# First attention's context as one fp32 product a block instead of three f16 ones

## The reference

```python
q = heads(hidden_states @ Wq.T + bq)
k = heads(hidden_states @ Wk.T + bk)
v = heads(hidden_states @ Wv.T + bv)
q = apply_rope(q)
k = apply_rope(k)
scores = jnp.einsum('bhqd,bhkd->bhqk', q, k) / jnp.sqrt(jnp.asarray(HEAD_DIM, q.dtype))
scores = jnp.where(causal[None, None], scores, jnp.finfo(scores.dtype).min)
weights = jax.nn.softmax(scores, axis=-1)
context = jnp.einsum('bhqk,bhkd->bhqd', weights, v)
merged = context.transpose(0, 2, 1, 3).reshape(B, S, INNER)
return merged @ Wo.T + bo
```

## Time and profile before

| | |
|---|---|
| median of 3 runs | 2036.06 us |
| profiled execution, its own time | 2036.67 us |
| its span, first to last instruction | 2034.0 us |
| mean granted TensorE clock | 0.95 |
| busy: TensorE products, VectorE, ScalarE, GpSimd | 87%, 72%, 57%, 28% |
| first attention's units | about 78 to 957 us of the span |

### The profile page before, as it was taken

One profiled execution on the slowest core, in us unless ns is written; L12 is line 12 of the kernel. 1 busy time (PEld: TensorE's weight loads), 2 busy tenths in 40 slices (PEclk: granted clock), 3 DMA queues, 4 the chain that ended last, 5 costly groups with the idle time before them and its releaser, 6 DMA issues. The chain is left out here.

```text
span 2034.0 us, 46207 instructions
## 1 busy us (share of the span) xinstructions
PE 1759.8 (87%) x15316; PEld 1102.3 (54%) x15316; DVE 1459.2 (72%) x3038; ACT 1157.2 (57%) x2198; POOL 559.5 (28%) x486
## 2 busy tenths in 40 slices
PE   3899999999999999997284789989989999973897
PEld 1577777777777777775142324444444444432455
DVE  4577777777777777776755587778788878825574
ACT  4566666666666666664565325555555555555453
POOL 1555545555545555541311500000000000002011
PEclk9999999999999999999597879999999999986899
DMA  4212211112211111210001000000000000001000
GB/s 127 83 46 50 49 44 47 42 42 49 49 38 47 43 41 47 49 40 3 0 1 64 1 1 1 2 1 0 0 0 0 0 0 0 1 1 62 1 21 21
DMA packets 47508, 56.67 MB, mean 28 GB/s; under 512 B 8337, under 2 KB 29010, under 8 KB 47442
## 3 DMA queue, kind: packets, MB, share of 16 engines
q1 hardware_dynamic: 47442, 55.82, 10.6%
HBM read 20.15 MB, written 2.10 MB: 11 GB/s over the span
## 5 line engine op out<-in xcount | busy, mean ns | idle before, releaser
L1622 ACT ACTIVATE a_prob<-psum 128x768 f32<-128x768 f32 (+5 forms) x384 | 303.7, 810 | 270.3 <-PE psum L1588 146.4
L1658 DVE TENSOR_REDUCE a_mx<-psum 128x1 f32<-128x512 f32 (+3 forms) x608 | 380.7, 659 | 78.0 <-PE psum L1530 48.9
L224 POOL TENSOR_TENSOR x<-x,y (+1 forms) x64 | 54.4, 880 | 980.1 <-ACT y L196 980.1
L1527 PE MATMUL psum<-a_kd,a_qp 128*128 128x512 f16 (+3 forms) x768 | 242.8, 340 | 36.5 <-DVE a_mx L1658 30.0
L1553 PE MATMUL psum<-a_qf,a_kd 128*128 128x512 f16 (+3 forms) x768 | 209.2, 327 | 4.0 <-ACT a_prob L1622 4.0
L528 POOL TENSOR_TENSOR a_swp<-a_swp,a_sin 128x512 f32<-128x512 f32 x128 | 163.4, 1276 | 162.8 <-DMA a_swp<-a_lin 157.9
L1527 PEld LDWEIGHTS psum<-a_kd,a_qp 128*128 128x128 f16 x768 | 73.9, 97 | 226.5 <-DVE a_mx L1658 176.0
L884 DVE TENSOR_REDUCE a_nmax<-psum 128x1 f32<-128x1024 f32 (+7 forms) x256 | 190.8, 746 | 0.6 <-PE psum L599 0.6
L532 POOL TENSOR_TENSOR a_rope<-a_swp,a_cosd 128x512 f32<-128x512 f32 x128 | 164.1, 1282 | 12.4 <-POOL a_swp L528 4.8
L879 DVE TENSOR_TENSOR a_pt_lo_big<-psum,a_pt_hi_big 128x512 f16<-128x512 f32 (+3 forms) x256 | 138.5, 581 | 30.8 <-ACT a_pt_hi_big L751 30.1
L756 ACT ACTIVATE a_prob_big<-psum,a_nmax 128x1024 f32<-128x1024 f32 (+3 forms) x128 | 121.7, 951 | 67.9 <-DVE a_nmax L884 64.6
(11 more groups left out here) (264 smaller groups left out, 4737.4 us busy)
## 6 DMA issues: line engine op xcount, KB each, us to landing
a_swp<-a_lin SPq DMA_DIRECT2D x256, 128.0 KB, 2.3
x<-_attn_hidden_states_dram SPq DMA_DIRECT2D x4, 512.0 KB, 5.5
a_w_raw<-in_L_attn_Wq_dram SPq DMA_DIRECT2D x16, 128.0 KB, 2.2
a_w_raw<-in_L_attn_Wk_dram SPq DMA_DIRECT2D x16, 128.0 KB, 2.3
a_w_raw<-in_L_attn_Wv_dram SPq DMA_DIRECT2D x16, 128.0 KB, 2.2
a_wo_raw<-in_L_attn_Wo_dram SPq DMA_DIRECT2D x1, 2048.0 KB
out_dram<-x SPq DMA_DIRECT2D x4, 512.0 KB, 2.9
f_raw<-in_L_ffn_w_dram SPq DMA_DIRECT2D x2, 704.0 KB, 5.1
```

Of the source, the lines that this page charges most:

```text
L1527: last = pe.matmul(work(slot, i * n, i * n + n), qp[:, wb, t * P:(t + 1) * P], kd[:, wb, j0 + i, a:e], start=True, stop=not edge)
L1622: act.activation(dst, src, ACT.Exp, scale=SCALE).then_inc(prob_ready, 1)
L1658: dve.tensor_reduce(mx[:, t, j0:j0 + per, p0], work(slot, 0, per * n).rearrange("p (j n) -> p j n", j=per), AX.X, ALU.max).then_inc(work_f ...
```

## The change

The turned probabilities and the values are kept in fp32, and `context` makes one fp32 product for each block instead of three f16 ones. A turned chunk leaves PSUM once: chunks of an even number by ScalarE (`even_chunk`), those of an odd number by VectorE (`odd_chunk`), each with its own semaphore, for which `turn` and `context` then wait. The values leave PSUM once, by ScalarE (`vals_out`); VectorE's `vals_lo` is gone. The room in SBUF is the same.

```diff
-        v_hi, v_lo = sb("v_hi", [P, 2, TB, HD0], F16), sb("v_lo", [P, 2, TB, HD0], F16)
+        v_all = sb("v_all", [P, 2, TB, HD0])
-        pt_hi = [sb("pt_hi_big", [P, 2, S], F16), sb("pt_hi_small", [P, 2, BANK], F16)]
-        pt_lo = [sb("pt_lo_big", [P, 2, S], F16), sb("pt_lo_small", [P, 2, BANK], F16)]
+        prob_t = [sb("prob_t_big", [P, 2, S]), sb("prob_t_small", [P, 2, BANK])]
...
                 def turn(u, b, p):
                     for at, j0, j1 in chunks(p):
-                        wait(pe, pt_lo_done, NC * u + at - 1)
+                        wait(pe, (pt_even, pt_odd)[at % 2], NC // 2 * u + at // 2)
...
                     for at, j0, j1 in chunks(p):
-                        pe.wait_ge(pt_lo_done, NC * u + at + 1)
+                        pe.wait_ge((pt_even, pt_odd)[at % 2], NC // 2 * u + at // 2 + 1)
                         for j in range(j0, j1):
-                            cols = slice(j * P, (j + 1) * P)
-                            for m, (vv, pp) in enumerate(((v_hi, pt_hi), (v_lo, pt_hi), (v_hi, pt_lo))):
-                                last = pe.matmul(dst, vv[:, b, j, :], pp[p % 2][:, (p // 2) % 2, cols],
-                                                 start=(j == 0 and m == 0), stop=(j == BLOCKS[p] - 1 and m == 2))
+                            last = pe.matmul(dst, v_all[:, b, j, :], prob_t[p % 2][:, (p // 2) % 2, j * P:(j + 1) * P],
+                                             start=(j == 0), stop=(j == BLOCKS[p] - 1))
...
-                def vals_hi(v, b, i):
+                def vals_out(v, b, i):
-                    act.activation(v_hi[:, b, 4 * i:4 * i + 4, :], work(VALS_SLOT[i], 0, BANK).rearrange("p (t n) -> p t n", t=4),
-                                   ACT.Copy, scale=1.0 / WSCALE).then_inc(vhi_ready, 1)
+                    act.activation(v_all[:, b, 4 * i:4 * i + 4, :], work(VALS_SLOT[i], 0, BANK).rearrange("p (t n) -> p t n", t=4),
+                                   ACT.Copy, scale=1.0 / WSCALE).then_inc(v_ready, 1)
...
-                def turned_hi(u, b, p):
+                def even_chunk(u, b, p):
                     for at, j0, j1 in chunks(p):
-                        act.wait_ge(turned, NC * u + at + 1)
-                        if j0 == 0:
+                        if at % 2 == 0:
+                            act.wait_ge(turned, NC * u + at + 1)
                             wait(act, ctx_made, 8 * u + p - 3)
-                        act.activation(pt_hi[p % 2][:, (p // 2) % 2, j0 * P:j1 * P], c.psum[:, turned_bank(at), 0:(j1 - j0) * P],
-                                       ACT.Copy).then_inc(pt_hi_done, 1)
+                            act.activation(prob_t[p % 2][:, (p // 2) % 2, j0 * P:j1 * P], c.psum[:, turned_bank(at), 0:(j1 - j0) * P],
+                                           ACT.Copy).then_inc(pt_even, 1)
...
-                def vals_lo(v, b, i):
-                    dve.wait_ge(vhi_ready, 2 * v + i + 1)
-                    dve.scalar_tensor_tensor(out=v_lo[:, b, 4 * i:4 * i + 4, :],
-                                             in0=work(VALS_SLOT[i], 0, BANK).rearrange("p (t n) -> p t n", t=4), scalar=1.0 / WSCALE,
-                                             in1=v_hi[:, b, 4 * i:4 * i + 4, :], op0=ALU.mult, op1=ALU.subtract).then_inc(v_ready, 1)
...
-                def turned_lo(u, b, p):
+                def odd_chunk(u, b, p):
                     for at, j0, j1 in chunks(p):
-                        dve.wait_ge(pt_hi_done, NC * u + at + 1)
-                        cols = slice(j0 * P, j1 * P)
-                        dve.tensor_tensor(pt_lo[p % 2][:, (p // 2) % 2, cols], c.psum[:, turned_bank(at), 0:(j1 - j0) * P],
-                                          pt_hi[p % 2][:, (p // 2) % 2, cols], ALU.subtract).then_inc(pt_lo_done, 1)
+                        if at % 2 == 1:
+                            dve.wait_ge(turned, NC * u + at + 1)
+                            wait(dve, ctx_made, 8 * u + p - 3)
+                            dve.tensor_copy(prob_t[p % 2][:, (p // 2) % 2, j0 * P:j1 * P],
+                                            c.psum[:, turned_bank(at), 0:(j1 - j0) * P]).then_inc(pt_odd, 1)
```

More of the change, by code:

```diff
@@ L432, in attention_0 @@
         sin_done, rope_ready, rhi_ready, qk_ready = sem("sin_done"), sem("rope_ready"), sem("rhi_ready"), sem("qk_ready")
-        vals_made, vhi_ready, v_ready = sem("vals_made"), sem("vhi_ready"), sem("v_ready")
+        vals_made, v_ready = sem("vals_made"), sem("v_ready")
         scored, max_done, exp_done = sem("scored"), sem("max_done"), sem("exp_done")
-        turned, pt_hi_done, pt_lo_done = sem("turned"), sem("pt_hi_done"), sem("pt_lo_done")
+        turned, pt_even, pt_odd = sem("turned"), sem("pt_even"), sem("pt_odd")
         ctx_made, ctx_hi_done, ctx_lo_done = sem("ctx_made"), sem("ctx_hi_done"), sem("ctx_lo_done")
@@ L767, in unit @@
                         if p < 7:
-                            turned_hi(u, b, p + 1)
+                            even_chunk(u, b, p + 1)
                         elif exists(u + 1):
-                            turned_hi(u + 1, 1 - b, 0)
+                            even_chunk(u + 1, 1 - b, 0)
                         if p == 0 and exists(u + 1):
@@ L793, in unit @@
                         if p == 2 and exists(u + 1):
-                            vals_hi(u + 1, 1 - b, 0)
+                            vals_out(u + 1, 1 - b, 0)
                         if p == 3 and exists(u + 1):
-                            vals_hi(u + 1, 1 - b, 1)
+                            vals_out(u + 1, 1 - b, 1)
                             rope_hi(u + 1, 1 - b, 3)
@@ L813, in _ @@
                 rope_hi(0, 0, 1)
-                vals_hi(0, 0, 0)
-                vals_hi(0, 0, 1)
+                vals_out(0, 0, 0)
+                vals_out(0, 0, 1)
                 rope_hi(0, 0, 2)
@@ L829, in _ @@
                                ACT.Copy, scale=WSCALE).then_inc(const_ready, 1)
-                turned_hi(0, 0, 0)
+                even_chunk(0, 0, 0)
                 exponent(0, 0, 2)
@@ L895, in unit @@
                         if p < 7:
-                            turned_lo(u, b, p + 1)
+                            odd_chunk(u, b, p + 1)
                         elif exists(u + 1):
-                            turned_lo(u + 1, 1 - b, 0)
+                            odd_chunk(u + 1, 1 - b, 0)
                         if p < 5:
@@ L914, in unit @@
                             add_out(u - 1, h - 1 + b, 1 - b, 3)
[L915 to L918, removed]
                         if p == 2 and b == 0 and exists(u + 2):
@@ L937, in _ @@
                     cosine(0, 0, i)
-                vals_lo(0, 0, 0)
-                vals_lo(0, 0, 1)
                 dve.wait_ge(wohi_ready, 1)
@@ L949, in _ @@
                 cosine(1, 0, 2)
-                turned_lo(0, 0, 0)
+                odd_chunk(0, 0, 0)
                 maximum(0, 0, 2)
```

## The result

The changed kernel takes 2068.09 us (median of 4 runs, 2067.24 to 2069.99), against 2035.93 for the kernel before (4 runs): a ratio of 1.0159, 95% interval 1.0141 to 1.0176. It is slower, by 32 us; forecast were 2071 and 34. The span grew from 2034.0 to 2066.7 us.

A forecast was written before the change was run, and what follows sets the result against it. TensorE's start-to-start product times were taken to bound the first attention. On 2036.7 us, 60.5 + 3.1 − 23.8 − 2.4 − 3.0 = +34.4 gave 2071 us; 8-in-10 range 2056 to 2104, own case 2058 to 2088.

The forecast's parts named there:

- products: Context blocks on TensorE: 1152 blocks at 220 ns each in place of 167.5, +60.5 us.
- bare first loads: Contexts of steps 2 and 3, behind values of 128 f16 columns: first weight load uncovered by about 50 ns, +3.1 us.
- wait for `y`: Step 2, values' product waiting for VectorE: 0.80 us lost 30 times, taken as gone, −23.8 us.
- step-5 score behind GpSimd: Step-5 score, 0.08 us late behind five turns for GpSimd's low part, 30 times: gone, −2.4 us.
- last unit: Last unit, without projections or values as cover: one eviction instead of two shortens TensorE's idle time, −3 us (0 to 5).
- Two records a product: Each fp32 product of 128 columns runs as two records, 110 ns each, 220 ns a block.
- the third neighbour, L633: Source line with 128-column weight loads in the old trace, read as a load holding the way for 104 to 110 ns.
- the turns' 110 ns a record: Pace of the fp32 one-record turns of 128 columns, taken as the pace of each context record.
- Loads covered: Context stream on TensorE: each load of 104 to 110 ns is just covered by a product of 108 to 110 ns.
- Rival 1: Context loads not covered by products: a block costs 436 ns, total 2317 us; chance 8%.
- the two causes that were named: At step 2, one copy replaces two low parts on VectorE (0.38 us earlier); TensorE comes 0.47 us later.
- ScalarE's relief as a margin: ScalarE no longer handles each chunk before `a_lin`, which VectorE's cosine waits for; without it the margin is 0.05 us.

The follow-up runs named there:

- The first run: Kernel before, three f16 products a block, with step 1's output addition that frees the bank moved ahead of the maximum: 2035.4 us, ratio 0.9995.

## Why the prediction was right

It named the right side, the size and the mechanism: +34.4 us by its sum, +32.2 between the medians. By its terms:

| term | forecast | measured | from |
|---|---|---|---|
| products | +60.5 | 1152 x (223.2 − 167.5) = +64.2 | the records' pace, 111.6 ns |
| bare first loads | +3.1 | 60 x 0.052 = +3.1 | the two contexts above |
| wait for `y` | −23.8 | −23.8 | no such wait left |
| step-5 score behind GpSimd | −2.4 | −2.4 | no such wait left |
| last unit | −3.0 | −4.2 (idle from 930 to 962 us: 8.8; after, from 961 to 996: 4.6) | stretches |
| ahead of the loop | none | −2.0 (first turn at 75.69 for 76.86, and 0.8 less idle up to 95 us) | timeline, stretches |

The measured terms make +34.9. The stage's last product starts at 994.87 instead of 960.18 us, +34.7. What comes behind it is 2.1 us shorter, 1071.8 against 1073.8, work that the change doesn't touch; where these 2 us come from wasn't tried. In the traces of this study the first turn starts anywhere from 74.9 to 77.6 us, and what comes behind the stage's last product lasts 1068.8 to 1075.0, so neither these 2 us nor the first turn's 1.2 can be called an effect of the change. The forecast is nearer than its terms deserve: they are 3.7 us too low for the products, and the last unit and these two differences make up for it.

- *Two records a product.* Right, and so was the third neighbour, L633: a load of 104 to 110 ns. The mis-sized term is the pace: I took the turns' 110 ns a record, whose loads have records of 141 ns against 192 here. The load is longer than its product, by some 2 ns, and with 2304 records that made the sum 3.7 us too low. The run with half the columns shows that the load sets the pace, the run with half the weights that the product would allow 110.
- *Loads covered.* Rival 1 is out: whole-array loads of 192 ns lie under products 112 ns apart. The Trainium skill, "TensorE: Matmul & The Clock Gate", Part 3, The mechanism, has a line that loads overlap products in flight only when the row group differs; taken without the background buffer, which the same section names too, that doesn't agree with this trace. The run with half the weights shows a case in which they don't overlap: where the width changes. The Terms of that page of the Trainium skill give transpose mode as four times faster for fp32. This trace has twice: a block costs 223 ns and a turn 110.
- *The wait for `y` goes.* Right, and by the two causes that were named, at 0.46 us each; 0.38 was forecast for the copy because I priced it at 0.69 from its record, and its pace is 0.60. I also counted on ScalarE's relief as a margin. The run with all chunks on VectorE shows none of it. The step-5 score's 2.4 us went as forecast, but of the two reasons given only TensorE's lateness is borne out: with single evictions and three f16 products the score still starts some 0.07 us late behind its turns in each unit, with double evictions and fp32 products it never does.
- *What the prediction didn't see.* It took the wait for `y` as the only thing between TensorE and its pace. The first run shows another close behind it: with the addition moved ahead of the maximum, TensorE waited as long for low parts of chunks. The forecast was safe from this because the change has no late maximum and relieves the evictions as well. The prediction had not asked, so that is luck.
- *The range's own ends.* They don't follow from the terms. 216 ns a block with every wait gone makes some 2066 us, not 2058; loads that stick out by 5 ns make 2083, half of the wait for `y` left makes the same, and neither 2088. The forecast doesn't rest on them.

So the change joined a gain and a loss. By the ratios its evictions are worth 23 us by themselves (with the low parts left out), 33 with the addition moved. Its product costs 64, and 3 for the bare first loads, and hides a part of what the evictions give.

## What to carry to other kernels

Where one engine has no idle time left, price a product by the distance between starts, and take weight loads into it: an fp32 product of 128 columns is two records, each as long as its 128-column load, and costs a third more than the three f16 products that it replaces. A wait that stands alone in the chain of waits isn't therefore the only one. Before its length goes into a sum, ask which other resource the engine would reach too early, and what the cure itself makes late; here the same edit was worth 0, 10 and 19 us, by what stood behind it. Two reliefs of the same wait add up only until it is gone, so test them alone and together.

## What the runs showed of the hardware

- Changing the width of the weights between 128 and 64 columns in a stream of fp32 products costs time, on the way down and on the way up: 60 us over the kernel for two switches in each of 6 rows in 32 units, 0.16 us a switch (about 0.14 down and 0.20 up in the row shown). Narrower weights made the kernel slower.
- Halving the moving columns of an fp32 product under 128-column weights shortens only one step of a row, that behind the first narrow record, to 56 ns; the loads stay 112 ns apart.
- The last twelve products of the stage, behind a gap of 2.26 us, ran in the kernel after with records of 0.40 and 0.42 us from the third on, against 0.27 in the kernel before, where the same gap stood ahead of them; the twelve starts take 2.13 us against 1.22. The granted clock from 993.0 to 995.3 us is 0.50 there, which is the level of 1.2 GHz; in the kernel before it is 1.00 from 958.9 to 960.5. Why it fell in one and not in the other isn't shown.
